# A fused decoder of four gated layer pairs on one core: the mLSTM by chunks of 128 tokens with a carried state, and five ternary weights quantised in the expert loop

## The reference

```python
# mLSTM, for each batch and head
ig, fg = x3 @ Wi + bi, x3 @ Wf + bf          # x3 = [q, k, v], 768 features
F      = cumsum(log_sigmoid(fg))             # over tokens
log_D  = F[s] - F[t] + ig[t]   for t <= s, -inf otherwise
D      = exp(log_D - max_t log_D)
C      = (q @ k.T / sqrt(16)) * D
h      = C / (max(|sum_t C|, exp(-max log_D)) + 1e-6) @ v
out    = (h - mean(h)) * rsqrt(var(h) + 1e-6) * ln_scale
# ternary weights of the two feed-forward layers, five of 1024 x 256
scale  = mean(|w|) + 1e-5 ;  wq = clip(round(w / scale), -1, 1)
```

## Time and profile before

| what | us |
|---|---|
| three runs | 657.25, 658.81, 660.98 (median 658.81) |
| span of the profiled execution | 652.8 |
| TensorE busy | 501.9 (77%) |
| VectorE busy | 389.4 (60%) |
| ScalarE busy | 275.4 (42%) |
| GpSimd busy | 144.4 (22%) |
| granted TensorE clock, mean | 0.872 |

### The profile page before, as it was taken

The page is one execution under the profiler, slowest core; times in us unless marked ns, Lnnn a source line. Parts: engine busy times, 40 slices in busy tenths (PEclk is TensorE's granted clock), DMA queues, the critical chain, the costliest instruction groups (busy, mean ns, idle before and its releaser), DMA issues.

```text
span 652.8 us, 7578 instructions
## 1 busy us (share of the span) xinstructions
PE 501.9 (77%) x2570; PEld 347.6 (53%) x2578; DVE 389.4 (60%) x1083; ACT 275.4 (42%) x512; POOL 144.4 (22%) x138
## 2 busy tenths in 40 slices
PE   2999886869997237876777879999997766755674
PEld 1788752358883113434344445788884444633442
DVE  6544368911111556766567558522459899999844
ACT  1100144112321134478597741233456762334765
POOL 4000037790005763000303123000023011011200
PEclk9999977969999565887899976999999997965867
DMA  8880011026977170299994000000000000000000
GB/s 283 268 307 2 0 39 57 18 59 221 334 180 136 44 101 5 52 261 219 106 120 124 2 1 1 2 0 1 1 0 1 1 1 1 1 1 0 17 21 28
DMA packets 52886, 49.14 MB, mean 75 GB/s; under 512 B 7070, under 2 KB 45092, under 8 KB 52848
## 3 DMA queue, kind: packets, MB, share of 16 engines
q1 hardware_dynamic: 49776, 44.92, 29.0%
q0 software_dynamic: 3072, 3.75, 2.2%
HBM read 40.71 MB, written 12.58 MB: 82 GB/s over the span
## 4 chain that ended last, share of the span: by engine, by line
PE 38%; DVE 28%; issue 8%; DMA 7%; ACT 6%; SPq 6%; POOL 6%; POOLq 0%; DVEq 0%; ACTq 0%
PE bank L1338 5%; PE bank L1420 4%; PE bank L1348 4%; DVE big L1045 3%; SPq L390 3%; PE bank L1599 3%; POOL xg_rows L510 3%; PE bank L1442 2%; DVE top L1048 2%; DMA SH<-query_parts 2%; DVE bnst L576 2%; PE bank L1613 2%; PE bank L1638 2%; PE bank L1622 2%; DMA query_parts<-ar 2%
## 5 line engine op out<-in xcount | busy, mean ns | idle before, releaser
L470 POOL TENSOR_TENSOR rstd<-ve,neghalf 128x2 f32<-128x2 f32 x32 | 25.7, 804 | 260.8 <-DVE ve L581 260.6
L863 DVE SCALAR_TENSOR_TENSOR HM<-bank,HM 128x384 f32<-128x384 f32 x64 | 35.6, 556 | 50.0 <-ACT HM L1187 41.4
L1185 ACT ACTIVATE HM<-bank,ATN 128x256 f32<-128x256 f32 x64 | 31.3, 490 | 40.3 <-PE bank L1522 39.6
L537 POOL DMA_INDIRECT WK<-y_rows,slot x32 | 33.3, 1039 | 66.5 <-DMA y_rows<-ph 53.9
L1533 PE MATMUL bank<-HM 128*32 128x256 f32 x128 | 43.4, 423 | 4.1 <-ACT HV L1169 2.3
L1320 PE MATMUL bank<-identf,HN 128*128 128x128 f32 x96 | 18.2, 327 | 33.7 <-DVE HN L586 33.6
L1515 PE MATMUL bank<-CMP,sel 96*128 96x256 bf16 x64 | 19.2, 300 | 31.2 <-DVE HM L863 14.1
L546 POOL TENSOR_TENSOR rs<-vr,neghalf 128x32 f32<-128x32 f32 x4 | 22.1, 5522 | 94.8 <-DVE vr L847 94.8
L1072 ACT ACTIVATE HT<-bank 128x512 f32<-128x512 f32 x24 | 14.0, 598 | 67.4 <-PE bank L1320 67.4
L741 DVE TENSOR_TENSOR he<-sil,bank 64x64 f32<-64x64 f32 x32 | 7.0, 219 | 54.4 <-ACT sil L1119 54.2
L510 POOL DMA_INDIRECT xg_rows<-HN,slot x32 | 32.8, 1026 | 21.6 <-DVE slot L707 12.5
(11 more groups left out here) (293 smaller groups left out, 1262.3 us busy)
## 6 DMA issues: line engine op xcount, KB each, us to landing
...
```

The source lines that it names most:

```text
L470: pool.tensor_tensor(rstd[:, b, :], ve[:, b, :], neghalf[:, 0:TB], ALU.pow)\
L537: pool.indirect_dma_start(out=G4[:, q, k, :], out_offset=None, in_=y_dram, in_offset=bass.IndirectOffsetOnAxis(slot[:, t, k:k + 1], 0), bo ...
L863: dve.scalar_tensor_tensor(out=dcs[:, 2 + i % 3, :], in0=bank[4 + i % 2][:, 0:384], scalar=DH ** -0.5, in1=dcs[:, i % 2, :], op0=ALU.mult, ...
L1185: act.activation(dcs[:, i % 2, 0:S], bank[2 + i % 2][:, 0:S], ACT.Exp, bias=ATN[:, 0, 32 * b + h:32 * b + h + 1])
```

## The change

**The mLSTM.** Decays are centred on the maximum at token 127 of each batch. The key half 0 to 127 acts on the query half 128 to 255 as a state: `weighted_values` and `states` build 16 x 17 blocks, `block_states` masks them, `inter` multiplies them by the later queries and `earlier_part` weights the result. Within each half, the 128 x 128 causal block is computed as before, but for two heads at once: 512 columns, two heads by two halves. `exponents` makes the whole exponent in PSUM (mask, minus the maximum of the query row, plus the key term), so that one Exp (`decays`) does without a bias. `scores` uses float32 directly, with the key's 32 features (two heads) as the rows of the product and queries of which the other head is set to zero (QM, made by `queries_copy`). Four row groups write four banks. `values` has four heads beside each other on 32 columns of the array each. Every product that isn't a score or a value (a JOB) goes by turns into banks 4 and 5. key_parts, query_parts and all their transfers are gone. The values are centred beforehand, so the head norm needs no mean; its last two multiplications are on GpSimd.

**The weights.** They are loaded in the expert loop to `ar`, by turns into two halves. Row t = 3w of ScalarE has the Abs passes of weight w, row 3w + 1 of TensorE the totals, row 3w + 2 the rounding (ScalarE) and two clips (VectorE). The ring of expert chunks is three. The gate weights for k and v are added first, so that context gates take half the products.

The diff, cut to its core:

```diff
-        CH, RING = 2, 4
+        CH, RING = 2, 3
...
+        JOBS = [("turn", 0), ("gates", 0), ("rows", 0)]
+        for o_ in range(NO):
+            b_, k_ = o_ // 2, o_ % 2
+            JOBS.append(("D", 4 * o_))
+            if k_ == 1:
+                JOBS.append(("state", b_))
+            if k_ == 0 and b_ in (0, 1):
+                JOBS.append(("turn", b_ + 1))
+            JOBS.append(("D", 4 * o_ + 1))
+            if (o_, 1) == (0, 1):
+                JOBS.append(("gates", 1))
+            if o_ == 2:
+                JOBS.append(("turn", 3))
+            JOBS.append(("D", 4 * o_ + 2))
+            if k_ == 1:
+                JOBS.append(("inter", b_))
+            if o_ == 2:
+                JOBS.append(("gates", 2))
+            if o_ in (1, 3):
+                JOBS.append(("rows", (o_ + 1) // 2))
+            JOBS.append(("D", 4 * o_ + 3))
+            if k_ == 0 and b_ >= 2:
+                JOBS.append(("turn", B + b_ - 2))
+        JOBS.append(("turn", B + 2))
+        READ_BY_V = ("gates", "state", "inter")
...
+        RAW = [ar[:, 2048 * (i % 2):2048 * (i % 2 + 1)] for i in range(NQ)]
+        QWS = [m.bitcast(BF16) for m in (WK2[:, 0:1024], WK2[:, 1024:2048], big[:, 9216:10240], big[:, 10240:11264],
+                                         big[:, 11264:12288])]
...
+            def load_weights(w):
+                sp.dma_start(pair(RAW[w], a[QNAMES[w]].shape[0] // P), rows_of(QNAMES[w]))\
+                    .then_inc(loads[QNAMES[w]], 16)
...
+                w = (t + 2) // 3
+                if w >= 2 and (t + 2) % 3 == 0 and w < NQ:
+                    sp.wait_ge(s["s_qw"], w - 1)
...
-            stack(1, KST[1], kp_dram, 1)
-            store_queries(0)
-            stack(0, QST[0], qp_dram, 0)
-            sp.wait_ge(s["s_gx"], NT)
-            store_queries(1)
-            stack(1, QST[1], qp_dram, 0)
...
+                pool.tensor_tensor(hh, HRJ[:, :, 0:DH], rs[:].unsqueeze(2).broadcast_to([P, TB * NH, DH]), ALU.mult)\
+                    .then_inc(s["s_hh"], 1)
+                pool.wait_ge(s["s_hh"], 2 * b + 1)
+                pool.tensor_tensor(pair(hhf), pair(hhf), lns[:].unsqueeze(1).broadcast_to([P, TB, D]), ALU.mult)\
+                    .then_inc(s["s_hh"], 1)
...
+                if t % 3 == 1 and w < NQ:
+
+                    dve.wait_ge(s["s_xgT"], t + 1)
+                    link(dve.tensor_tensor(wsc[:, w:w + 1], wt[:, 2 * w:2 * w + 1], wt[:, 2 * w + 1:2 * w + 2], ALU.add))
+                    link(dve.tensor_scalar(wsc[:, w:w + 1], wsc[:, w:w + 1], 1.0 / (NI * D), 1e-5, ALU.mult, ALU.add))
+                    dve.reciprocal(wrec[:, w:w + 1], wsc[:, w:w + 1]).then_inc(s["s_wsc"], 1)
+                if t % 3 == 2 and w < NQ:
+
+                    dve.wait_ge(s["s_wr"], w + 1)
+                    link(dve.tensor_scalar(QWS[w], RAW[w], -MAGIC, 1.0, ALU.add, ALU.min))
+                    dve.tensor_scalar(QWS[w], QWS[w], -1.0, None, ALU.max).then_inc(s["s_qw"], 1)
...
+            for i in range(4 * NO):
+                o, g, b, at = i // 4, i % 4, i // 8, i % 8
+                dve.wait_ge(s["s_sc"], 4 * o + 2 * (g // 2) + 2)
+                dve.wait_ge(s["s_freea"], read_before(job("D", i))[1])
+                if o >= 1:
+                    dve.wait_ge(s["s_pv"], 2 * (o - 1) + g // 2 + 1)
+                dve.tensor_tensor(cs[:, g, :], bank[g][:], dcs[:, i % 2, :], ALU.mult).then_inc(s["s_cs"], 1)
+                if i in (0, 1, 6, 8):
+                    t = 4 + (0, 1, 6, 8).index(i)
+                    if i == 1:
+                        gate_rows(1)
+                    gathered(t)
+                    if t % 2 == 1:
+                        ln_stats(t // 2)
+                if i in (3, 12):
+                    sum_rows(1 + (3, 12).index(i))
+                if i in (4, 13):
+                    max_rows(1 + (4, 13).index(i))
+                if i in (5, 14):
+                    part_rows(1 + (5, 14).index(i))
+                if i in (3, 9):
+                    token_norm(2 + (3, 9).index(i))
+                if i == 10:
+                    gate_rows(2)
+                if at == 3:
+                    weighted_values(b)
+                if at == 5:
+                    block_states(b)
+                if b >= 1 and at == 4:
+                    heads_sum(b - 1)
+                if b >= 1 and at == 6:
+                    heads_var(b - 1)
+                if at == 6:
+                    earlier_part(b)
+                if b >= 2 and at == 1:
+                    heads_add(b - 2)
+                if b >= 2 and at == 2:
+                    heads_norm(b - 2)
+            heads_add(B - 2)
+            heads_norm(B - 2)
+            heads_sum(B - 1)
+            heads_var(B - 1)
 
             def add_scaled(b, src):
...
-                    for last in range(4, 6):
-                        heads_norm(b, last)
+                    heads_add(b)
...
+                if t % 3 == 0 and w < NQ:
+
+                    landed(act, QNAMES[w])
+                    for h in range(2):
+                        cols = slice(NI * h, NI * (h + 1))
+                        last = act.activation(QWS[w][:, cols], RAW[w][:, cols], ACT.Abs,
+                                              accum_out=asum[:, 2 * w + h:2 * w + h + 1])
+                    last.then_inc(s["s_asum"], 1)
+                if t % 3 == 2 and w < NQ:
+
+                    act.wait_ge(s["s_wsc"], w + 1)
+                    act.activation(RAW[w], RAW[w], ACT.Identity, bias=magic[:, 0:1], scale=wrec[:, w:w + 1])\
+                        .then_inc(s["s_wr"], 1)
+
...
+            act.preload_act_table_set("natural_log_exp_and_others")
...
+            def queries_copy(b):
+
+                act.wait_ge(s["s_job"], job("turn", b) + 1)
+                src = pair(job_bank("turn", b)[:])
+                act.activation(HT[:, :, S * b:S * (b + 1)], src, ACT.Copy)
+                if b >= 3:
+                    act.wait_ge(s["s_sc"], 8 * (b - 2))
+                for par in range(2):
+                    last = act.activation(QM[b % 3][:, :, par, :], src, ACT.Identity, scale=pm[:, par:par + 1])
+                last.then_inc(s["s_freea"], 1)
+
...
+            def decays(i):
+
+                act.wait_ge(s["s_job"], job("D", i) + 1)
+                if i >= 2:
+                    act.wait_ge(s["s_cs"], i - 1)
+                act.activation(dcs[:, i % 2, :], job_bank("D", i)[:], ACT.Exp).then_inc(s["s_freea"], 1)
+
...
-                if SUMS <= i < SUMS + NW:
-
-                    w = i - SUMS
-                    landed(act, ("q2g", "q2u", "q2d", "q3a", "q3b")[w // 2])
-                    act.activation(half(QWS, w), half(RAW, w), ACT.Abs, accum_out=asum[:, w:w + 1])\
...
+                if t % 3 == 1 and t // 3 < NQ:
+
+                    w = t // 3
+                    pe.wait_ge(s["s_asum"], w + 1)
+                    last = pe.matmul(bank[q][:, 400:402], onesf[:], asum[:, 2 * w:2 * w + 2], start=True, stop=True)
...
+            def exponents(i):
+
+                b, o, g = i // 8, i // 4, i % 4
+                h = 8 * (o % 2) + 2 * g
+                dst = job_free("D", i)
+                pe.wait_ge(s["s_cmp"], min(b, 2) + 1)
+                view = dst[:].rearrange("p (t a n) -> p t a n", t=TB, a=2)
+                pe.matmul(dst[:], identb[:], future[:, 0:P].unsqueeze(1).broadcast_to([P, 4, P]), start=True, stop=True)
+                for par in range(2):
+                    pe.matmul(view[:, :, par, :], nsel[0:96, h + par, :], CMP[0:96, b, 0:S], start=False, stop=True,
+                              skip_group_check=True)
+                for t in range(TB):
+                    last = pe.matmul(dst[:, S * t:S * (t + 1)], CMP[0:96, b, S + P * t:S + P * (t + 1)],
+                                     sel[0:96, h:h + 2, :], start=False, stop=True, skip_group_check=True)
+                last.then_inc(s["s_job"], 1)
...
+            def scores(o, gs):
+
+                b, k = o // 2, o % 2
+                if k == 0:
+                    pe.wait_ge(s["s_freea"], read_before(job("turn", b))[1])
+                if o >= 1:
+                    pe.wait_ge(s["s_cs"], 4 * (o - 1) + gs[-1] + 1)
...
+                for t in range(TB):
+                    for g in gs:
+                        r = slice(32 * g, 32 * (g + 1))
+                        q = S * b + P * t
+                        last = pe.matmul(bank[g][:, S * t:S * (t + 1)], CT[r, k, q:q + P],
+                                         QM[b % 3][r, k, :, P * t:P * (t + 1)], start=True, stop=True)
+                        if t == TB - 1:
+                            last.then_inc(s["s_sc"], 1)
+
...
+            def values(o, pg):
+
+                b, k = o // 2, o % 2
+                pe.wait_ge(s["s_cs"], 4 * o + 2 * pg + 2)
+                if b >= 1 and k == 0 and pg == 0:
+                    pe.wait_ge(s["s_hrc"], b)
+                for t in range(TB):
+                    for j in range(4):
```

(13 more changed lines are left out.)

657 lines of the change are left out of this document (313 added, 344 removed), and 1 row of the table names.

## The result

The changed kernel takes 663.27 us (median of 4, 662.84 to 667.38) against 658.03 for the kernel before: a ratio of 1.0113, 95% interval 1.0061 to 1.0165. It is slower by about 1%, where 620 was forecast. Its profiled span is 661.1 us (652.8 before), with a mean granted clock of 0.827 (0.872).

A forecast was written before the change was run, and what follows sets the result against it. Stages had different limits: TensorE nearly full in the expert loop and after 395.93 us, no engine full in the mLSTM loop. +8.0 (holding the expert loop's +13.5) - 54.7 + 7.6 = -39.1, from 658.8 to 620; range 606 to 638.

The forecast's parts named there:

- 63 / 0.76 = 83: mLSTM loop: TensorE's 63 us of work divided by an assumed busy share of 0.76 gives 83 us.
- Term 1: Expert loop: quantising makes TensorE wait 12.6 us for Abs sums, total +13.5 us, bounds 0 and 25.
- Term 2: From expert loop to first head pair: first decay product at 253.8, +8.0 us, expert-loop delay included.
- Term 3: mLSTM loop: 82 us against 136.7, so -54.7 us; bounds 63 and 123.
- the 82: mLSTM loop: its forecast length in us, against 136.7 before.
- Term 4: End of the mLSTM loop: low-rank products 21 us after the last product, against 13.4; +7.6 us, bounds 0 and 12.
- Starvation: Expert loop: weights come too late; +12 us more, 632, inside the range; chance included in the forecast's 0.63.
- Tiles one by one: mLSTM loop: TensorE's tiles do not overlap; loop 112 us, time 649; chance 0.14.
- The slower rival: mLSTM loop: TensorE stays at the lower clock; loop 134 to 140 us, time 672 to 678; chance 0.07.
- near no change: Whole kernel: a time between the one-by-one and the lower-clock outcomes; chance 0.03.

The follow-up runs named there:

- Experiment 3: 36 products that add no result put ahead of TensorE's wait for the Abs sums in five expert-loop rows of the changed kernel; 657.24 us, ratio 1.0035.
- the last version: Last two gathered tiles moved behind the fourth score product, against the version with early reads, rows ahead, late totals and root on ScalarE; 605.54 us, ratio 0.9248.

## Why the prediction was wrong

Two steps failed: the time was lost to a stall priced at its own length in the expert loop, and to "63 / 0.76 = 83" in the mLSTM loop. Against the forecast span of 613.7 the profile has 661.1: 47.4 us, of which 9.4 stand before the loop, 40.8 in it, and -2.8 behind.

**Term 1, quantising in the expert loop: the stall right, the clock left out.** 12.6 us of waits were forecast and 9.5 came; VectorE's and ScalarE's added work cost nothing else. That order decides and not rate was right. What failed is that a stall was priced at its own length. After three of the four long waits the clock fell to its lower level, and the products of the stage took 14.0 us more. Experiment 3 shows it apart: with the wait filled the loss in the profile is 12.3 us, near the +13.5 of the term, and no drop of the clock follows. The profile before had the warning: 0.50 from 245 to 260 after gaps. I used it for the mLSTM loop and not here.

**Term 2, up to the first decay product: right.** It came 42.4 us behind the last output copy, for which the term had 43.8 (253.8 less 196.5 + 13.5). From the end of batch 0's norm it was 17.7 us for the forecast 18.5. The 9.4 us of delay are the 10.8 that term 1 missed, less 1.4.

**Term 3, the loop: the work right, the efficiency wrong.** TensorE's work was forecast at 63 us; in the window from 267 to 387 it is 84.84 us busy at a clock of 0.72, thus some 61 at full clock (64 over the 125 us of the four windows shown with the result). VectorE's was 62 and is 59.37. The overlap of tiles, the doubtful point, held: values 1.02 us and scores 2.0 at half clock, where each would need 3.5 one by one. The failed step is "63 / 0.76 = 83", which took the share of the loop before for one that any loop of this kind has. It left 20 us for waits and low clock together. There were 59: 35 of waits, 24 of low clock.

Part of that is an error inside the step, which no experiment was needed to find. The 63 us are work at full clock, but the 0.75 of the earlier trace rows is busy time at a mean clock of 0.82, so the share of full-clock work there is 0.61, and 63 / 0.61 is 103 us. Over the whole loop before:

```profile
245.00:384.00 139.00, 106.38 (x642) 58.48 (x642) 91.65 (x202) 94.44 (x205) 24.47 (x12) 0.88 0.60 104
```

That gives 0.67 and 94 us. The low clock was thus left out of this term as well, 11 to 20 of the 40.8 us.

The rest is order. The old loop had 64 short steps, and TensorE waited for VectorE there only at the product of scores and decay (L863, 15.9 us), for none of its small operations; the new one puts the carried state's two reads, the weighting and the gate rows of three groups between 32 long steps, and I priced these as 0.43 us of VectorE each without asking what is queued behind them. What the order costs is shown: reads ahead of the score product -9.7 us, weights and rows ahead -7.6, the root on ScalarE -3.5, gathered tiles behind -9.7, together 30.5 of the 119.2 us by profiles of one execution each. Counted as in the forecast, from the first decay product, the last version's loop is 92.6 us for 122.8, still 10.6 over the 82, and the turn and gate products of batch 1 have gone ahead of it. That this structure can reach 82 is not shown; that the changed kernel's order does was the error.

What the low clock alone is worth in the loop stays partly open. Fillers raised it from 0.71 to 0.83 at no change of time. The sums fit a full price for it behind the first wait (some 8 us given back for 10.6 spent), but no run raised the clock without adding work, and none tried fillers at the entry with the wait for the gathered tiles gone.

**Term 4, the end of the loop: right in sum, in part by luck.** 20.5 us against 21. Two parts are off and cancel: the last-but-one variance came 0.2 us before the loop's end and not 2, and the copies, sums and squares took 1.9 us and not 4.5. The power of 5.44 us and the two products behind it stand on the chain of waits of the kernel after:

```profile
385.81 5.44 POOL ar L558
391.25 0.07 issue
391.32 1.06 POOL ar L560
392.38 0.07 issue
392.45 1.27 POOL ar L563
```

**The rivals.** Starvation didn't come. Tiles one by one is refuted by the rows of L1654 and L1639; the Trainium skill (TensorEngine Tiling (Array Packing), Gotcha 1) asks for separate banks for row tiles, and these scores, in two banks, overlap (2.0 us for 3.5). The slower rival was to decide at a loop of 121 us; the loop was 122.8, so the outcome is at its edge, with the low clock it named in 24 us of it. But it needed a mean clock below 0.56, the mean was 0.72, and the waits did the rest. It had 0.07 and stood for 672 to 678; the measured 663.27 lies between that and "near no change", which had 0.03, and the range ended at 650. The two costs, waits and clock, were treated as one alternative each, though in the expert loop the second followed from the first.
